# Softmax denominators of a cross-attention kernel: VectorE's reciprocal of a whole PSUM tile in place of a gather, a small reciprocal and a broadcast through DRAM

## The reference

```python
def xattn(Q, K, V, mask, W_q, W_k, W_v, W_o):          # B=4, Sq=1024, Sk=2048, D=512, 16 heads of 32
    q, k, v = heads(Q @ W_q.T), heads(K @ W_k.T), heads(V @ W_v.T)
    scores = einsum('bhqd,bhkd->bhqk', q, k) / sqrt(32)
    e = where(mask, exp(clip(scores, -50, 50)), 0)
    attn = e / sum(e, axis=-1)                          # the denominators of this study
    return merge(einsum('bhqk,bhkd->bhqd', attn, v)) @ W_o.T

x = x + xattn(layernorm(x), ctx, ctx, mask, W_q, W_k, W_v, W_o)
x = x + int8_ffn(layernorm(x), rhs)                     # rows and columns quantised to int8, product, scales
```

## Time and profile before

| what | value |
|---|---|
| time, median of 3 runs | 1904.02 us (1899.14 to 1912.62) |
| the profiled execution: its own time | 1900.09 us |
| its span in the trace | 1898.2 us |
| granted TensorE clock, mean | 0.981 |
| busy PE, DVE, ACT, POOL | 93%, 71%, 69%, 17% |

### The profile page before, as it was taken

One profiled execution on the slowest core, in us unless ns is written; L12 is line 12 of the kernel. 1 busy time (PEld: TensorE's weight loads), 2 busy tenths in 40 slices (PEclk: granted clock), 3 DMA queues, 4 the chain that ended last, 5 costly groups with the idle time before them and its releaser, 6 DMA issues.

```text
span 1898.2 us, 30520 instructions
## 1 busy us (share of the span) xinstructions
PE 1762.8 (93%) x10845; PEld 1007.4 (53%) x10872; DVE 1348.2 (71%) x1552; ACT 1310.4 (69%) x1713; POOL 322.4 (17%) x169
## 2 busy tenths in 40 slices
PE   6988999999999998999999999999999999999986
PEld 5985555546455565655555565555655333333333
DVE  4546777766777777778776777877777767676855
ACT  4446777767776776767677676777767777777742
POOL 0000010100112121222103122211311212121213
PEclk9999999999999999999999999999999999999997
DMA  6685555555465555646556564565646454636232
GB/s 236 203 218 155 133 144 132 159 127 150 124 157 148 142 166 135 182 117 178 143 141 171 129 189 117 147 167 137 185 114 166 111 138 97 151 89 150 56 118 100
DMA packets 224543, 276.31 MB, mean 146 GB/s; under 512 B 27136, under 2 KB 141824, under 8 KB 223744
## 3 DMA queue, kind: packets, MB, share of 16 engines
q1 hardware_dynamic: 224384, 274.28, 54.2%
HBM read 181.41 MB, written 92.54 MB: 144 GB/s over the span
## 4 chain that ended last, share of the span: by engine, by line
PE 51%; issue 14%; DVE 11%; DMA 11%; POOL 6%; ACT 5%; SPq 2%; POOLq 0%; ACTq 0%; DVEq 0%
PE tile L788 17%; PE scores L810 14%; PE wsum L826 13%; DMA denoms<-recip_row 8%; DVE acc L1260 7%; ACT probs L996 3%; POOL rstd L1322 3%; PE scores L788 2%; POOL sums L1301 2%; PE tile L853 2%; PE tile L847 1%; SPq L753 1%; DMA recip_row<-recip_c 1%; DMA v_parts<-v_stage 1%; POOL normed L1335 1%
## 5 line engine op out<-in xcount | busy, mean ns | idle before, releaser
L996 ACT ACTIVATE probs<-scores 128x1024 f32<-128x1024 f32 x1024 | 991.8, 1023 | 265.9 <-PE scores L810 263.6
L1260 DVE TENSOR_TENSOR acc<-acc,probs 128x2048 f32<-128x2048 f32 x376 | 892.0, 2372 | 172.1 <-ACT probs L996 158.5
L810 PE MATMUL scores<-q_stack,k_stack 128*128 128x512 f32 x2048 | 616.3, 419 | 55.1 <-ACT probs L996 54.3
L810 PEld LDWEIGHTS scores<-q_stack,k_stack 128*128 128x128 f32 x2048 | 348.4, 189 | 420.9 <-ACT probs L996 272.7
L826 PE MATMUL wsum<-probs,v_sb 128*32 128x512 f32 x4096 | 515.8, 611 | 0.0
L1322 POOL TENSOR_TENSOR rstd<-var_eps,minus_half 128x1 f32<-128x1 f32 x56 | 93.6, 1672 | 863.2 <-DVE var_eps L1159 863.2
L826 PEld LDWEIGHTS wsum<-probs,v_sb 128*32 128x32 f32 x4096 | 104.8, 110 | 243.5 <-issue 221.1
L1211 DVE TENSOR_TENSOR squares<-squares 128x128 bf16<-128x128 bf16 x160 | 39.7, 248 | 156.2 <-ACT squares L1036 155.9
L1301 POOL TENSOR_TENSOR sums<-sums,denoms 128x512 f32<-128x512 f32 x32 | 76.4, 2389 | 401.8 <-DMA denoms<-recip_row 401.8
L1260 DVE TENSOR_TENSOR acc<-probs 128x2048 f32<-128x2048 f32 x32 | 73.4, 2293 | 82.8 <-ACT probs L996 82.8
L788 PE MATMUL tile<-ctx_hi,wk_hi 128*128 128x256 f32 x412 | 115.6, 281 | 1.8 <-DVE ctx_lo L1169 1.8
(11 more groups left out here) (192 smaller groups left out, 1890.4 us busy)
## 6 DMA issues: line engine op xcount, KB each, us to landing
k_stack<-k_parts SPq DMA_DIRECT2D x256, 256.0 KB, 5.8
q_stack<-q_parts SPq DMA_DIRECT2D x128, 256.0 KB, 6.6
v_parts<-v_stage SPq DMA_DIRECT2D x64, 256.0 KB, 4.7
v_sb<-v_parts SPq DMA_DIRECT2D x64, 256.0 KB, 4.6
raw<-ctxT SPq DMA_DIRECT2D x28, 512.0 KB, 4.2
k_parts<-stage_hi SPq DMA_DIRECT2D x96, 128.0 KB, 2.0
k_parts<-stage_lo SPq DMA_DIRECT2D x96, 128.0 KB, 2.0
k_parts<-q_stack SPq DMA_DIRECT2D x64, 128.0 KB, 4.2
```

The source lines that it names most:

```text
L810: last = nc.tensor.matmul(scores[:, h, :], k_stack[:, kt // 4, h, (kt % 4) * P:(kt % 4 + 1) * P], q_stack[:, qb, h, :], start=True, stop=True)
L996: nc.scalar.activation(probs[:, slot % RING, 2 * pair:2 * pair + 2, :], scores[:, 2 * pair:2 * pair + 2, :], ACT.Exp, scale=1.0 / math.sqr ...
L1260: nc.vector.tensor_tensor(acc[:, :, :], other, probs[:, slot % RING, :, :], ALU.add).then_inc(sems["add_done"], 1)
```

## The change

DVE reads the whole `dsum` tile from PSUM, takes its reciprocals (128x512) and writes them to `denoms`, in the pair of slots in which the half ends, after the row work of that pair. Gone are ACT's copy, the gather, the 128x16 reciprocal, the store and the broadcast load. PE's wait for the bank and POOL's wait for the reciprocals are both on the new instruction (`recips_ready`).

```diff
@@ SP
-                        if slot == first + 3:
-                            ct.wait_alone(sp, "denoms_copied", k)
-                            sp.dma_start(den_c[:, :], denoms[0:P:DH, :]).then_inc(sems["denoms_spread"], 16)
-                        if slot == first + 6:
-                            ct.wait_alone(sp, "recips_ready", k)
-                            sp.dma_start(recip_row.rearrange("h (a j) -> (h a) j", j=G * QB // P), recip_c[:, :]).then_inc(sems["recips_stored"], 16)
-                        if slot == first + 7:
-                            ct.wait_alone(sp, "recips_stored", 16 * k)
-                            sp.dma_start(denoms[:, :], recip_row[:, None, :].broadcast_to((G, DH, QB))) \
-                                .then_inc(sems["recips_loaded"], 16)
@@ PE, sums_of, denoms_of and piece (three places)
-                            ct.wait(pe, "denoms_copied", half)
+                            ct.wait(pe, "recips_ready", half)
...
-                                ct.wait(pe, "denoms_copied", int(slot > KT))
+                                ct.wait(pe, "recips_ready", int(slot > KT))
@@ ACT, half_done
-                    ct.wait(act, "denoms_full", k)
+                    ct.wait(act, "step_summed", KT * k)
                     ct.wait(act, "o_stored", 32 * (k - 1))
-                    nc.scalar.copy(denoms[:, :], dsum).then_inc(sems["denoms_copied"], 1)
-                    ct.wait(act, "step_summed", KT * k)
                     nc.scalar.copy(sums[:, :], wsum[:, :]).then_inc(sems["sums_copied"], 1)
@@ DVE, at the end of each pair of slots
                     for first, k, on in ((0, 0, seg.prev), (KT, 1, seg.b)):
-                        if on and even == first + 4:
-                            ct.wait(dve, "denoms_spread", 16 * k)
-                            nc.vector.reciprocal(recip_c[:, :], den_c[:, :]).then_inc(sems["recips_ready"], 1)
+                        if on and even == first:
+                            ct.wait(dve, "denoms_full", k)
+                            ct.wait(dve, "o_stored", 32 * (k - 1))
+                            nc.vector.reciprocal(denoms[:, :], dsum).then_inc(sems["recips_ready"], 1)
@@ POOL, normalise
-                ct.wait(pool, "recips_loaded", 16 * k)
+                ct.wait(pool, "recips_ready", k)
```

More of the change, by code:

```diff
@@ L251 @@
     "bound_gathered": lambda g: 16 * g.count("bound"),
-    "denoms_spread": (0, 32, 0), "recips_stored": (0, 32, 0), "recips_loaded": (0, 32, 0),
     "scores_full": (0, 64, 0), "step_summed": (0, 32, 0), "acc_summed": (0, 2, 0), "denoms_full": (0, 2, 0),
@@ L259 @@
     "v_copied": lambda g: g.count("V"), "qT_copied": lambda g: g.count("T"), "scale_copied": lambda g: g.count("R"), "rhs_copied": lambda g: g.count("U"),
-    "denoms_copied": (0, 2, 0), "sums_copied": (0, 2, 0),
+    "recips_ready": (0, 2, 0), "sums_copied": (0, 2, 0),
     "norms_read": lambda g: 2 * g.count("N"), "bound_ready": lambda g: g.count("bound"), "flag_ready": lambda g: g.count("flag"),
     "add_done": lambda g: 2 * g.adds * g.b, "ctx_split": lambda g: g.count("split"), "lo_done": lambda g: g.count("K", "Q", "X"),
-    "recips_ready": (0, 2, 0),
     "dve_chain": lambda g: 2 * g.count("stats", "O") + 4 * g.count("quant"), "var_ready": lambda g: g.count("stats", "O"), "xn_ready": lambda g: g.count("apply"),
@@ L314, in program @@
         o_parts = nc.dram_tensor("o_parts", (B * G, 2, P, SQ), F32).ap()
-        recip_row = nc.dram_tensor("recip_row", (G, QB), F32).ap()
         w_hi = {n: sb(f"w{n}_hi", [P, KC, D], F32R) for n in "qkvo"}
@@ L355, in program @@
         o_hi = denoms[:, :].bitcast(F32R)
-        den_c = sb("den_c", [P, G * QB // P])
-        recip_c = sb("recip_c", [P, G * QB // P])
         w_amax = sb("w_amax", [P, KC])
```

## The result

The changed kernel takes 1918.3 us (median of 11 runs, 1915.36 to 1920.36) against 1905.83 us for the kernel before (11 runs, 1897.16 to 1912.62). The forecast was 1924, with a range from 1905 to 1950. The profiled execution has a span of 1916.6 us (before 1898.2) and a mean granted clock of 0.974 (before 0.981).

A forecast was written before the change was run, and what follows sets the result against it. PE, busy 93%, was taken to bound the kernel. Losses 31.2 + 7.4 + 5.9 + 7.7 + 0.5 less 32.2 gained gave 20.5 us slower: 1920.6 from the profiled 1900.1, 1924 as median; range 1905 to 1950.

The forecast's parts named there:

- The instruction's length: The new 128x512 DVE reciprocal takes r = 3.3 us, range 2.9 to 4.7, from three narrower reciprocals in the trace.
- The round trip goes: PE no longer loses time behind the DRAM round trip of the reciprocals: 32.2 us gained.
- Place 1: Second boundary, passes 4 to 11: PE's V piece waits for the bank, 3.9 us late eight times, 31.2 us lost.
- Place 2: Second boundary, passes 0 to 3: PE waits for the bank, 1.84 us late four times, 7.4 us lost.
- Place 3: First boundary, passes 4 to 11: PE's O piece waits for the bank, 0.74 us late eight times, 5.9 us lost.
- Passes 12 to 14: Second boundaries: DVE runs 2.55 us later, POOL, ACT and PE follow; three times, 7.7 us lost.
- ACT's copy, SP and the DMAs at 0: Removing ACT's 32 copies of `dsum` and the three DMAs with their waits on SP gains nothing.
- The tail: Tail's loads of x up to 2.5 us late, POOL's last multiplication spared a 2.29 us wait: net 0.5 us lost.
- nothing is late next: the multiplication starts when POOL reaches it: First boundaries: POOL's multiplication no longer waits and ACT finds it done, so the whole 32.2 us is gained.
- What waits for it: PE may not write bank 6 until `recips_ready`; scores and ACT's exponentials stand behind; three places, 31.2, 7.4 and 5.9 us.
- The rival of absorption: DVE gains on PE during stalls, 12 `x_in` waits vanish: 1904 to 1912 us; chance 0.25 together with r below 3.0.

The follow-up runs named there:

- experiment 2: Changed kernel, but ACT's copy of dsum returns and frees the bank; DVE takes the reciprocal in SBUF at the same place in its stream: 1917.71 us, ratio 1.0061.
- experiment 3: Changed kernel, with PE computing the K tile of slot 18 three times over in passes 4 to 11, ahead of the V piece: 1912.53 us, ratio 1.0028.
- experiment 7: Changed kernel, with POOL's multiplication at first boundaries of passes with stage C waiting until DVE has quantised: 1905.09 us, ratio 0.9995.
- experiment 5: As experiment 2, but at second boundaries the reciprocal stands in slot 24, behind the row work and ahead of slot 25's addition: 1891.42 us, ratio 0.993.
- 8: As experiment 2, but the second boundary's reciprocal stands two pairs later, at the end of slots 20 and 21, behind `x_in`: 1879.41 us, ratio 0.9866.
- 9: As experiment 2, second-boundary reciprocal after slots 20 and 21 (slot 24 in passes 12 to 14), plus POOL's wait for quantisation at first boundaries: 1856.54 us, ratio 0.973.
- experiment 1: Changed kernel, with DVE copying the denominators in place of the reciprocal, the output then multiplied by them: 1865.02 us, ratio 0.9784.

## Why the prediction was right, and what it had wrong

**The direction held, and the time lies in the range.** The sum was +20.5 us against the profiled execution; the spans differ by 18.4, the medians by 12.5 (the kernel before spreads over 15 us, and its profiled execution lies 5.7 us below its median). That the sum comes so near the 18.4 is in part luck, as the terms below show.

- *The instruction's length* (3.3): 3.35. The narrow rows were enough; the rise from 3.0 to 6.0 ns an element did not go on (from 16 to 512 elements it is 6.3). The Trainium skill's repeat count ("VectorE: DVE Perf Modes", "First, the fixed hardware budget"), from which I had estimated 4.3 us, does not give the time here.
- *The round trip goes* (32.2 gained at PE): those stalls are 0 after. Right. The small stalls at the ends of passes 3, 7 and 11 (3.3 in all), which I had set apart as another place, went too; why was not tried.
- *Place 1* (31.2): 8 x 3.7 = 29.8. *Place 2* (7.4): 4 x 1.6 = 6.4. *Place 3* (5.9): 8 x 0.5 = 3.9. The three make up the 40.1 us of the new row.
- *Passes 12 to 14* (7.7): the stall grew from 3.2 to 5.65 three times, +7.4. But the stage lost 11.1: the wait for `q` there, 1.2 before and 2.1 after, adds 2.8, and the granted clock of the stage went from 0.98 to 0.95, which no experiment took apart.
- *ACT's copy, SP and the DMAs at 0*: experiment 2 brings the copy back and leaves the time where it was (1917.71 to 1918.3), which agrees. The DMAs were not tried alone.
- *The tail* (0.5): pass 15 and the tail together came out 2.5 us shorter, not 0.5 longer. Open: PE's waits for `v_sb` in the tail, 10.6 us before and 9.3 after, are 7.1 in experiment 3, which leaves that part of the kernel as the change has it.

**The step that failed is the gain's "nothing is late next: the multiplication starts when POOL reaches it".** It did start then, and beside it DVE's `x_in` (in passes 12 to 15 its `normed`) took 1.50 us in place of 0.55. PE's wait for `q` rose from 6.5 to 18.2 us, 11.7 that no term and no rival has; experiment 7 takes it away and is 13 us faster by the medians. Without it the change would have been level.

**"What waits for it" named the visible wait, not the cause.** I had PE held by `recips_ready` on the bank and made the sum there. Experiment 2 shows that this wait can be taken away and nothing is gained, and experiment 5 that the same instruction elsewhere in DVE's stream gives 26 us. The number came out since both waits measure the same lateness of DVE. As advice it would have been wrong: freeing the bank alone would have looked like the cure. It is a part of it, since the better places of experiments 5, 8 and 9 stand behind the V piece; no run moved the reciprocal with the bank still held.

**The rival of absorption happened in part, for another reason.** The waits for `x_in` went from 15.6 to 7.4 us. My rival had DVE gaining on PE, and the argument against it had everything moving along with PE. Neither: PE came later, because its clock was lower behind the stall (experiment 3). **The clock was in no term.** For passes 4 to 11, the 6.6 us behind each of the eight stalls lose 6.6 x (1 - clock): 18 us after (some 17 by experiment 3), 8.5 before, so +9.5; `x_in` gives back 8.2 of it (9.8 before, 1.6 after). The whole of that stage at PE is then 29.8 + 3.9 for the bank, +8.0 for `q`, +9.5 for the clock, -8.2 for `x_in`, -27.4 for `probs`: +15.6, where the stage lost 13.1. Two omissions of some 9 us that cancel, and one of 11.7 that was covered by terms forecast a little too large, by the small stalls that went, and by passes 0 to 3, which I had at +2.8 and which came out at -2.7: that is the luck in the sum. Why these four are quicker the traces tell. PE's waits for `probs` there fall from 14.8 to 9.4 us, those at the bank add 6.4, and the two stretches at the lower clock in passes 2 and 3 are gone, 2 x 6.6 x 0.25 = 3.3 us; together -2.3.

## What to carry to other kernels

When a long latency is taken out of a kernel of engines that run in step, ask not only which wait goes but what the freed engine now does at that moment, and beside whom. A long instruction on an in-order engine belongs behind the work that others wait for, not where its input becomes ready: the same 32 reciprocals made 1918 or 1857 us here, by their place (with the bank freed by a copy, which alone gave nothing) and one wait of POOL. And before freeing what an engine visibly waits for, look for the next thing that it needs from the same late engine.

## What the runs showed of the hardware

- A float32 reciprocal of 128x512 on DVE takes 3.35 us out of PSUM and 3.35 out of SBUF; a copy of the same tile out of PSUM takes 0.685 on DVE (experiment 1).
- After 3.7 us of idle PE in a stream that is busy before and behind, the granted clock is 0.54 to 0.75 over the next 6.6 us, eight times of eight; after 0.87 to 0.90 us at the same place (experiment 3) and after 1.05 (experiment 1), 1.00, eight times of eight each; after 2.8 to 3.3 us at another place (before, passes 4 to 11), 0.74 or 0.75 five times and 1.00 three times. After 2.26 us (before, passes 2 and 3) it is 0.75 and 0.74; after 1.61 us (after, passes 0 to 3), 1.00 four times of four.
- A DVE operation with one tensor in SBUF (128x512, `x_in`) takes 0.54 us alone and 1.50 beside POOL's multiplication of two tiles.
- That multiplication (128x512) takes 1.28 us beside `x_in` and 3.28 beside DVE's additions of two tensors in SBUF (experiment 7). The addition keeps its 2.29 us, and the 128x128 operation behind it takes 1.32 in place of 0.22. The rows look as if the two took turns; no run was made for that.
